# Causal attention: scores and maxima from float32r parts in two 64-row tiles of the array

## The chip, the cores and the metric

The program runs on one core of a Trainium2 chip. The metric is the device time of one execution in microseconds, here the median of three runs. The granted TensorE clock is given as a share of 2.4 GHz: 1.00 is 2.4 GHz and 0.50 is 1.2 GHz.

## What is computed

A stack of four stages over 1024 rows of 512 numbers: a mixture-of-experts layer, a causal attention layer, the same mixture-of-experts layer again, and two further layers. The change touches only the causal attention, whose core is

```python
q = _rope(q, cos, sin)
k = _rope(k, cos, sin)
k = jnp.repeat(k, Q_PER_KV, axis=2)          # 8 key heads serve 32 query heads
scores = jnp.einsum('bqhd,bkhd->bhqk', q, k) * SM_SCALE
scores = jnp.where(mask[None, None], scores, jnp.finfo(scores.dtype).min)
probs = jax.nn.softmax(scores, axis=-1)
ctx = jnp.einsum('bhqk,bkhd->bqhd', probs, v).reshape(B, S, HIDDEN)
```

with 1024 positions, a head width of 16, 8 groups of 4 query heads that share one key and one value head, and a mask that is plain causality at this length. All is float32.

## The kernel before

The causal layer has three blocks, each with one hand-written instruction stream for each engine and semaphores between them. The line numbers are those of the profile.

**The projection** (L1475 to L1676). TensorE makes the queries, keys and values, 128 features by 512 positions in a unit. Of 12 units, 10 hold queries or keys. Each is turned by its position (ScalarE, VectorE, `rotate` on TensorE, GpSimd's sum at L1505) and then split into three bfloat16 parts whose sum is the float32 value: ScalarE casts the first (L1596), GpSimd subtracts it (L1512), ScalarE casts the second (L1600), VectorE subtracts the third (`third`, L1642). SyncE writes the three parts to DRAM (`causal_parts`, L1486). After the seventh write it loads the first group's keys (L1492). The block ends for every engine when SyncE has seen all ten writes land (L1494).

**The core** (L1742 to L2035), a loop over the 8 groups. Scores are taken with six stacked products of parts: `Q_PART` and `K_PART` name the pairs, each of 16 rows, so a product contracts 96 rows. It needs the row maximum before the exponential, and takes every product twice:
- `maximum` (L1864), with the queries as weights: 128 queries by up to 512 keys into one of three banks `mx`; VectorE adds the causal mask and takes the maximum (L2016), or the plain maximum for keys that lie wholly before (L2011). 48 of these make a group.
- `split_maxima` (L1774 to L1788, GpSimd) negates the maxima and splits them into three bfloat16 parts; `turn_maxima` (L1872) transposes them; ScalarE copies them out (L1962); GpSimd's own queue puts them as rows 96 to 98 under the queries (L1794). The keys have ones there.
- `scores` (L1882), with the keys as weights: 128 keys by up to 512 queries, 99 rows, into one of three banks `sc`. ScalarE takes the exponential (L1977) into `prob`; where the block lies on the diagonal GpSimd sets the rest to zero (L1808).
- `values` (L1899): `prob` times the value head, float32, four heads side by side in four 32-column tiles of the array.

A group has 12 steps of four scores. The scores of group g and the maxima of group g + 1 stand in turn, and the values of the step before stand between the third and the fourth score:

```python
for h in range(QPK):
    scores(g, u, h)
    if more:
        maximum(g + 1, UPS * u + h)
    if h == 2 and u >= 1:
        values(g, u - 1)
```

The last group has no maxima to take (`more` is False). The maxima of group 0 stand alone ahead of the loop. TensorE and SyncE run the middle six groups in a hardware loop (`Fori`). SyncE loads a group's keys and queries into place in `ks` and `qs`, which hold all eight groups; the first group's queries are loaded by SyncE and ScalarE at the start of this block (`first_queries`, L1738), and the others follow one after the other as fast as they land (L1748, L1750).

**The output** product and residual follow in the third block.

Of the kernel before, what the change touches and what calls it, by code (L numbers as in the profile page):

```python
# [14 lines left out]
P = 128  # L15
# [1389 lines left out]
def causal_attention_layer(m, name, split):  # L1405
# [8 lines left out]
    Q_PART = (0, 0, 1, 0, 1, 2)  # L1414
    K_PART = (0, 1, 0, 2, 1, 0)
    STACK = len(Q_PART) * HD
    MROWS = 3
    with ExitStack() as outer:
# [3 lines left out]
        parts_dram = nc.dram_tensor(f"{name}_parts", [3, QK_ROWS, S], BF16, kind="Internal").ap()  # L1422
        v_all, ks, ident = m.v_all, m.ks, m.ident_half
        consts, stack_in, ones_done = sem("consts"), sem("stack_in"), sem("ones_done")
# [3 lines left out]
        with ExitStack() as ctx:  # L1428
# [3 lines left out]
            def pb(what, shape, dt=F32):  # L1432
# [13 lines left out]
            rest = [sb(f"rest{s}", [P, CH]) for s in range(2)]  # L1446
            NPB = 4
            part = [sb(f"part{s}", [P, 3, CH], BF16) for s in range(NPB)]
# [10 lines left out]
            turned_done, p1_done, rest_done, p2_done, p3_done = (  # L1459
                sem("turned_done"), sem("p1_done"), sem("rest_done"), sem("p2_done"), sem("p3_done"))  # L1460
# [7 lines left out]
            KEYS = [r for r, n in enumerate(TURN) if n % FEATS == 0]  # L1468
            HALF_T = T // NCH
# [5 lines left out]
            with nc.Block() as block:  # L1475
                @block.sync
                def _(sp):
                    sp.dma_start(b_qkv[:, :], m.dram["b_qkv"]).then_inc(c_in, 16)
                    sp.dma_start(cos[:, :], m.dram["cos"]).then_inc(c_in, 16)
                    sp.dma_start(sin[:, :], m.dram["sin"]).then_inc(c_in, 16)  # L1480
                    m.clear_stale(sp)
                    for r, n in enumerate(TURN):
                        c, j = divmod(n, FEATS)
                        row = j * P
                        sp.wait_ge(p3_done, r + 1)
                        sp.dma_start(parts_dram[:, row:row + P, c * CH:(c + 1) * CH].rearrange("a p s -> p a s"),  # L1486
                                     part[r % NPB][:, :, :]).then_inc(part_out[r % NPB], 16)
# [9 lines left out]
                def _(pool):  # L1497
                    rstd_gpsimd(m, pool, nm)
                    for n in range(UNITS + 3):
                        if n - 1 in number:  # L1500
                            r = number[n - 1]
                            pool.wait_ge(sin_done, r + 1)
                            if r >= 2:
                                pool.wait_ge(rest_done, r - 1)
                            nc.gpsimd.tensor_tensor(turned[r % 2][:, :], with_cos[r % 2][:, :], with_sin[r % 2][:, :],  # L1505
                                                    ALU.add).then_inc(turned_done, 1)
                        if n - 2 in number:
                            r = number[n - 2]
                            pool.wait_ge(p1_done, r + 1)
                            if r >= 2:  # L1510
                                pool.wait_ge(p3_done, r - 1)
                            nc.gpsimd.tensor_tensor(rest[r % 2][:, :], turned[r % 2][:, :], part[r % NPB][:, 0, :],  # L1512
                                                    ALU.subtract).then_inc(rest_done, 1)
# [48 lines left out]
                def _(act):  # L1562
# [16 lines left out]
                    nc.scalar.copy(ident[:, :], m.ident[:, :]).then_inc(consts, 1)  # L1579
# [3 lines left out]
                    for n in range(UNITS + 4):  # L1583
# [7 lines left out]
                        if n - 2 in number:  # L1591
# [4 lines left out]
                            nc.scalar.copy(part[r % NPB][:, 0, :], turned[r % 2][:, :]).then_inc(p1_done, 1)  # L1596
                        if n - 3 in number:
                            r = number[n - 3]
                            act.wait_ge(rest_done, r + 1)
# [680 lines left out]
```

## Time and profile before

| | us |
|---|---|
| median of three runs | 1276.73 (1274.5 to 1277.15) |
| the profiled execution | 1276.3 |
| its span, first to last instruction | 1274.5 |
| mean granted TensorE clock | 0.924 |

The profile is of one execution. Its page gives each engine's busy time, the span in 40 slices and the costliest groups of instructions; its trace can be asked for a stretch (busy time of each engine, granted clock, share of the 16 DMA engines), for the instructions in order of time, and for who waited for whom. Matmuls are pipelined, so one lasts longer in the records than it holds the engine: what it holds is read from the distance between starts.

### The profile page before, as it was taken

The numbers are of one execution on the slowest core, as the hardware profiler recorded it, in microseconds if no ns is written. First come the engines' busy times: TensorE is split into PE (matmuls) and PEld (weight loads), VectorE is DVE, ScalarE is ACT, GpSimd is POOL, SyncE is SP. The second block draws the span as 40 slices with busy tenths as digits, with TensorE's granted clock in tenths as the row PEclk, the third lists the DMA queues.
The fourth block names the chain that finished last, engine by engine and source line by source line (L and its number), as shares of the span: only waits on it lengthen the run. The fifth ranks groups of instructions, "written<-read, shape, count | busy, mean of one in ns | idle before, by whom it ended". The sixth has DMA issues, their size and how long they took to land. (4 is left out here: it accounts for less than half of the span.)

```text
span 1274.5 us, 21579 instructions
## 1 busy us (share of the span) xinstructions
PE 1097.4 (86%) x5654; PEld 717.9 (56%) x5655; DVE 905.9 (71%) x1775; ACT 704.8 (55%) x1218; POOL 566.7 (44%) x582
## 2 busy tenths in 40 slices
PE   4969999999194899999997787999999947878597
PEld 3847777777182233333333675677777735467454
DVE  5869888887575888888860666888888847444632
ACT  3238787887143177777775131787888824424142
POOL 4335666664556244443331225566666545140200
PEclk9979999999596599999998888999999977989889
DMA  9367899764615550000000183789995561000001
GB/s 351 114 220 185 218 243 286 174 114 60 192 50 155 104 99 19 1 1 1 1 1 1 63 309 111 236 196 258 275 222 103 83 156 67 1 1 1 0 1 66
DMA packets 62798, 151.01 MB, mean 118 GB/s; under 512 B 12224, under 2 KB 17024, under 8 KB 58240
## 3 DMA queue, kind: packets, MB, share of 16 engines
q1 hardware_dynamic: 37440, 95.17, 22.3%
q0 software_dynamic: 22592, 50.27, 20.3%
q10 hardware_dynamic: 2688, 4.65, 1.1%
q8 instruction: 34, 0.56, 0.2%
q14 instruction: 44, 0.36, 0.1%
HBM read 104.89 MB, written 44.97 MB: 118 GB/s over the span
## 5 line engine op out<-in xcount | busy, mean ns | idle before, releaser
L811 POOL DMA_INDIRECT moe_acc_rows<-xn,moe_token_of x94 | 208.0, 2213 | 146.3 <-ACT xn L886 131.1
L923 DVE TENSOR_TENSOR moe_w_lo<-moe_raw,moe_w_hi 128x1536 fp32r<-128x1536 f32 x94 | 165.4, 1759 | 62.9 <-ACT moe_w_hi L874 62.7
L1977 ACT ACTIVATE causal_prob<-causal_sc 128x512 f32<-128x512 f32 (+3 forms) x384 | 166.8, 492 | 70.3 <-PE causal_sc L1882 69.7
L874 ACT CAST moe_w_hi<-moe_raw 128x1536 fp32r x94 | 138.7, 1475 | 78.0 <-issue 76.4
L1864 PE MATMUL causal_mx<-ks,causal_qs 96*128 (+4 forms) x384 | 131.4, 353 | 23.0 <-DMA causal_qs<-causal_parts 16.5
L831 PE MATMUL moe_gu<-moe_w_hi,xt_hi 128*128 128x512 f32 x282 | 148.4, 526 | 0.6 <-DVE moe_w_lo L923 0.6
L1882 PE MATMUL causal_sc<-causal_qs,ks 99*128 (+3 forms) x384 | 120.2, 333 | 1.9 <-ACT causal_prob L1977 1.7
L831 PE MATMUL moe_gu<-moe_w_hi,xt_lo 128*128 128x512 f32 x282 | 111.8, 396 | 0.0
L831 PE MATMUL moe_gu<-moe_w_lo,xt_hi 128*128 128x512 f32 x282 | 110.9, 393 | 0.0
L826 PE MATMUL moe_gu<-moe_raw,xn 128*128 x188 | 98.0, 603 | 5.0 <-ACT moe_w_hi L874 5.0
L1808 POOL TENSOR_SCALAR_AFFINE_SELECT causal_prob<-causal_prob 128x512 f32<-128x512 f32 x64 | 40.9, 639 | 115.9 <-ACT causal_prob L1977 115.5
L1899 PE MATMUL causal_po<-causal_prob,causal_v_now 128*32 128x512 f32 (+3 forms) x768 | 81.8, 498 | 9.9 <-POOL causal_prob L1808 9.4
L1882 PEld LDWEIGHTS causal_sc<-causal_qs,ks 99*128 (+1 forms) x384 | 36.4, 97 | 88.9 <-ACT causal_prob L1977 36.7
L2011 DVE TENSOR_REDUCE causal_top_low<-causal_mx 128x1 f32<-128x512 f32 x128 | 80.7, 682 | 7.1 <-PE causal_mx L1864 6.7
L2016 DVE CUSTOM_DVE_ANT_0 causal_mx<-causal_mx,causal_no_later 128x512 f32<-128x512 f32 (+3 forms) x128 | 59.6, 519 | 28.1 <-PE causal_mx L1864 26.7
L1864 PEld LDWEIGHTS causal_mx<-ks,causal_qs 96*128 (+1 forms) x384 | 37.8, 99 | 71.0 <-issue 27.7
L831 PEld LDWEIGHTS moe_gu<-moe_w_hi,xt_hi 128*128 128x128 f32 x282 | 53.6, 190 | 34.1 <-issue 21.6
L105 POOL TENSOR_SCALAR var_eps<-mean_var 128x1 f32<-128x1 f32 x24 | 9.3, 387 | 140.5 <-DVE mean_var L91 140.5
L2016 DVE CUSTOM_DVE_ANT_0 causal_mx<-causal_mx,causal_no_later,causal_top_low 128x512 f32<-128x512 f32 (+3 forms) x128 | 65.3, 553 | 8.9 <-PE causal_mx L1864 8.9
L831 PEld LDWEIGHTS moe_gu<-moe_w_lo,xt_hi 128*128 128x128 f32 x282 | 53.8, 191 | 29.9 <-issue 21.6
L897 ACT CAST xt_hi<-moe_tx 128x384 fp32r<-128x384 f32 x94 | 45.2, 480 | 29.6 <-PE moe_tx L840 25.7
L831 PEld LDWEIGHTS moe_gu<-moe_w_hi,xt_lo 128*128 128x128 f32 x282 | 53.4, 189 | 12.3
(317 smaller groups left out, 2724.5 us busy)
## 6 DMA issues: line engine op xcount, KB each, us to landing
moe_raw<-in_w_gu SPq DMA_DIRECT2D x34, 1024.0 KB, 6.1
moe_raw<-in_w_down SPq DMA_DIRECT2D x34, 512.0 KB, 8.2
causal_qs<-causal_parts SPq DMA_DIRECT2D x45, 128.0 KB, 3.6
moe_acc_rows<-moe_zeros SPq DMA_DIRECT2D x2, 2304.0 KB, 14.7
moe_acc_rows<-x SPq DMA_DIRECT2D x18, 256.0 KB, 2.0
moe_xn_rows<-xn SPq DMA_DIRECT2D x2, 2048.0 KB, 10.7
x<-moe_acc_rows SPq DMA_DIRECT2D x16, 256.0 KB, 6.8
xn<-moe_acc_rows ACTq DMA_DIRECT2D x16, 256.0 KB, 7.2
```

The source lines that it names most:

```text
L811: pool.indirect_dma_start(acc_rows[a], bass.IndirectOffsetOnAxis(ap=token_of[:, b - 3:b - 2].bitcast(U32), axis=0), out_rows[(b - 3) % OUT ...
L826: nc.tensor.matmul(gu[s][:, :], xt_plain[s][:, k, :], raw[:, bass.ds(at + k * 2 * FI, 2 * FI)], start=(k == 0), stop=False)
L831: last = nc.tensor.matmul(gu[s][:, :], xt(half, s, k), part[s][:, k - PLAIN, :], start=False, stop=(k == KT - 1 and half is m.xt_lo))
L874: nc.scalar.copy(w_hi[1 - s][:, :, :], raw[:, bass.ds(at + SPLIT_AT, GU_COLS - SPLIT_AT)].rearrange("p (k n) -> p k n", k=SPLIT)).then_inc ...
L897: nc.scalar.copy(m.xt_hi[:, ks, tokens], tx[s][:, PLAIN * P:KT * P].rearrange("p (k c) -> p k c", k=SPLIT)).then_inc(tx_hi, 1)
L923: nc.vector.tensor_tensor(w_lo[1 - s][:, :, :], raw[:, bass.ds(at + SPLIT_AT, GU_COLS - SPLIT_AT)].rearrange("p (k n) -> p k n", k=SPLIT), ...
L1864: nc.tensor.matmul(mx[i % BANKS][:, 0:w], qs[0:STACK, bass.ds(at, P)], ks[0:STACK, bass.ds(gn * S + kc * CH, w)], start=True, stop=True).t ...
L1882: nc.tensor.matmul(sc[b][:, o:CH], ks[0:STACK + MROWS, bass.ds(g * S + kb * P, P)], qs[0:STACK + MROWS, bass.ds(g * QG + (h * S + c * CH + ...
L1899: last = nc.tensor.matmul(po[2 * HD * h:2 * HD * (h + 1), o:CH], v_now[:, kb, :], prob[u % 2][:, h, o:CH], start=(kb == 0), stop=(kb == (c ...
L1977: nc.scalar.activation(prob[u % 2][:, h, o:CH], sc[(u * QPK + h) % BANKS][:, o:CH], ACT.Exp, scale=SCALE).then_inc(exp_done, 1)
L2011: nc.vector.tensor_reduce(top_low[:, t - TC, h:h + 1], found, AX.X, ALU.max).then_inc(mx_read, 1)
L2016: nc.vector.tensor_tensor_reduce(found, found, no_later[:, CH - w:CH], 1.0, least, ALU.add, ALU.max, top[:, t, h:h + 1]).then_inc(mx_read, 1)
```

## The change

Queries and keys are now split into two parts instead of three. The parts are float32r (a float32 that TensorE takes in a reduced precision), and three products of parts are stacked instead of six, so the contraction is 48 rows (50 with the two rows of maxima). The stacks lie twice in the memory: rows 0 to 49 serve the scores, rows 64 to 111 the maxima, so the two kinds of product use the two halves of the array. Both `keys` and `qs` hold two groups instead of eight (`g % 2`). SyncE loads each stack for itself: the scores' stack of group g + 1 when group g - 1 has made its scores, the maxima's stack of group g + 2 when group g's maxima are made. All stacks of group 0, and the maxima's stack of group 1, are now loaded in the projection block. The loops over groups on TensorE and SyncE are written out; ScalarE keeps its loop. The maxima are split into two parts; they are turned as float32.

```diff
-    Q_PART = (0, 0, 1, 0, 1, 2)
-    K_PART = (0, 1, 0, 2, 1, 0)
-    STACK = len(Q_PART) * HD
-    MROWS = 3
+    Q_PART = (0, 0, 1)
+    K_PART = (0, 1, 0)
+    MROWS = 2
+    MAX_AT = 2 * HD
+    SCORE_ROWS = slice(0, 3 * HD + MROWS)
+    MAXIMA_ROWS = slice(64, 64 + 3 * HD)
+    IN_SCORES = (0, HD, 2 * HD + MROWS)
+    IN_MAXIMA = (64, 64 + HD, 64 + 2 * HD)
...
-        parts_dram = nc.dram_tensor(f"{name}_parts", [3, QK_ROWS, S], BF16, kind="Internal").ap()
+        parts_dram = nc.dram_tensor(f"{name}_parts", [2, QK_ROWS, S], F32, kind="Internal").ap()
...
+        def load_keys(eng, rows, g, done):
+            at = g % 2 * S
+            for a, row in enumerate(rows):
+                eng.dma_start(ks.bitcast(F32)[row:row + HD, at:at + S],
+                              parts_dram[K_PART[a], g * HD:(g + 1) * HD, :]).then_inc(done, 16)
...
-            part = [sb(f"part{s}", [P, 3, CH], BF16) for s in range(NPB)]
+            part = [sb(f"part{s}", [P, 2, CH], F32R) for s in range(NPB)]
...
-                            for a in range(len(Q_PART)):
-                                sp.dma_start(ks[a * HD:(a + 1) * HD, 0:S], parts_dram[K_PART[a], 0:HD, :]).then_inc(stack_in, 16)
+                            load_keys(sp, IN_MAXIMA, 0, for_maxima_in)
+                            load_keys(sp, IN_SCORES, 0, for_scores_in)
+                        if r == QUERIES[-1] + 1:
+                            for k in QUERIES:
+                                sp.wait_ge(part_out[k % NPB], 16 * (k // NPB + 1))
+                            load_queries(sp, IN_MAXIMA, 0, for_maxima_in)
+                        if r == len(TURN) - 1:
+                            load_queries(sp, IN_SCORES, 0, for_scores_in)
+                            sp.wait_ge(for_maxima_in, 16 * LOADS)
+                            load_keys(sp, IN_MAXIMA, 1, for_maxima_in)
+                            load_queries(sp, IN_MAXIMA, 1, for_maxima_in)
...
-                            nc.gpsimd.tensor_tensor(rest[r % 2][:, :], turned[r % 2][:, :], part[r % NPB][:, 0, :],
-                                                    ALU.subtract).then_inc(rest_done, 1)
+                            nc.gpsimd.tensor_tensor(part[r % NPB][:, 1, :], turned[r % 2][:, :], part[r % NPB][:, 0, :].bitcast(F32),
+                                                    ALU.subtract).then_inc(part_lo_done, 1)
...
-                            nc.scalar.copy(part[r % NPB][:, 1, :], rest[r % 2][:, :]).then_inc(p2_done, 1)
...
-                    def third(n):
-                        r = number[n]
-                        dve.wait_ge(p2_done, r + 1)
-                        nc.vector.tensor_tensor(part[r % NPB][:, 2, :], rest[r % 2][:, :], part[r % NPB][:, 1, :],
-                                                ALU.subtract).then_inc(p3_done, 1)
...
-            NEG_OPS = (4, 4)
+            NEG_OPS = (2, 2)
...
-                    for a in range(0, len(Q_PART), 2):
-                        first_queries(sp, a)
...
-                    with sp.Fori(1, KV) as g:
-                        sp.wait_ge(stack_in, g * (16 * LOADS) - 16 * LOADS // 2)
-                        load(g)
...
+                    for g in range(KV - 1):
+                        if g:
+                            sp.wait_ge(sc_done, g * NS * QPK)
+                        load(IN_SCORES, g + 1, for_scores_in)
...
+                        if g + 2 < KV:
+                            sp.wait_ge(mx_done, (g + 1) * NMU)
+                            load(IN_MAXIMA, g + 2, for_maxima_in)
...
-                        nc.tensor.matmul(mx[i % BANKS][:, 0:w], qs[0:STACK, bass.ds(at, P)],
-                                         ks[0:STACK, bass.ds(gn * S + kc * CH, w)], start=True, stop=True).then_inc(mx_done, 1)
+                        at = gn % 2 * QG + h * S + t * P
+                        key = gn % 2 * S + kc * CH
+                        nc.tensor.matmul(mx[i % BANKS][:, 0:w], q_r[MAXIMA_ROWS, at:at + P], k_r[MAXIMA_ROWS, key:key + w],
+                                         start=True, stop=True).then_inc(mx_done, 1)
...
-                        nc.tensor.matmul(sc[b][:, o:CH], ks[0:STACK + MROWS, bass.ds(g * S + kb * P, P)],
-                                         qs[0:STACK + MROWS, bass.ds(g * QG + (h * S + c * CH + o), CH - o)],
+                        nc.tensor.matmul(sc[b][:, o:CH], k_r[SCORE_ROWS, key:key + P], q_r[SCORE_ROWS, at + o:at + CH],
                                          start=True, stop=True).then_inc(sc_done, 1)
...
-                    with pe.Fori(1, KV - 1) as g:
-                        group(g, False, True)
-                    group(KV - 1, False, False)
+                    for g in range(KV):
+                        group(g, g == 0, g < KV - 1)
```

`load` in the new core block waits for the same stack's load before it, then calls `load_keys` and `load_queries` (three DMAs each). `load_queries` moves 64 rows of 4 KB for each of the three parts. `Q_PART` has three entries, so `LOADS` is 6.

The change moves DMA issues on SyncE. At the seam of projection and core, SyncE's order was (`causal_parts` is the DRAM copy of the parts; a row that ends in x3 is three issues):

```order
L1486 DMA causal_parts<-causal_part 128x3x512 x7
L1492 DMA ks<-causal_parts 16x1024 x6
L1486 DMA causal_parts<-causal_part 128x3x512 x3
L1475 UNCONDITIONAL_BRANCH
L1743 UNCONDITIONAL_BRANCH
L1738 DMA causal_qs<-causal_parts 16x4x1024 x3
L1757 DMA causal_no_later<-in_later 128x512
L1758 DMA causal_wd_raw<-in_w_dense 128x1024
```

and is now, where the second branch row again ends the projection block:

```order
L1511 DMA causal_parts<-causal_part 128x2x512 x7
L1440 DMA causal_keys<-causal_parts 16x1024 x6
L1511 DMA causal_parts<-causal_part 128x2x512
L1446 DMA causal_qs<-causal_parts 16x4x1024 x3
L1511 DMA causal_parts<-causal_part 128x2x512 x2
L1446 DMA causal_qs<-causal_parts 16x4x1024 x3
L1440 DMA causal_keys<-causal_parts 16x1024 x3
L1446 DMA causal_qs<-causal_parts 16x4x1024 x3
L1499 UNCONDITIONAL_BRANCH
L1749 UNCONDITIONAL_BRANCH
L1756 DMA causal_wd_raw<-in_w_dense 128x1024
```

The three queries' loads of the maxima moved from behind the block's end to behind the eighth write, and nine more issues stand between the last write and the block's end.

On GpSimd, at the head of the core block, the split of the maxima was

```order
L1774 TENSOR_SCALAR causal_neg<-causal_top 128x16
L1779 CAST causal_neg_parts<-causal_neg 128x4x4
L1782 TENSOR_TENSOR causal_left<-causal_neg,causal_neg_parts 128x16
L1785 CAST causal_neg_parts<-causal_left 128x4x4
L1788 TENSOR_TENSOR causal_neg_parts<-causal_left,causal_neg_parts 128x4x4
L1794 DMA causal_qs<-causal_neg_turned 1x4x512 x3
```

and is now

```order
L1777 TENSOR_SCALAR causal_neg<-causal_top 128x16
L1782 CAST causal_neg_parts<-causal_neg 128x4x4
L1785 TENSOR_TENSOR causal_neg_parts<-causal_neg,causal_neg_parts 128x4x4
L1791 DMA causal_qs<-causal_neg_turned 1x4x512 x2
```

two operations and one DMA shorter, twice in each group. TensorE's order of scores, maxima and values inside a group is the same as before.

## Rows read from the trace of the kernel before

**Rows 1.** The page: busy us (share of the span) xinstructions, by engine.
```profile
PE 1097.4 (86%) x5654; PEld 717.9 (56%) x5655; DVE 905.9 (71%) x1775; ACT 704.8 (55%) x1218; POOL 566.7 (44%) x582
```
**Rows 2.** Stretches: length, PE, PEld, DVE, ACT, POOL busy, clock, DMA share, GB/s.
```profile
409.92:438.93 29.01, 23.25 (x56) 5.55 (x57) 24.66 (x80) 0.57 (x1) 4.30 (x14) 0.50 0.62 123
...
627.32:658.73 31.41, 30.09 (x210) 11.34 (x209) 27.04 (x84) 22.32 (x52) 12.07 (x26) 1.00 0.01 1
658.73:686.60 27.87, 22.36 (x158) 6.63 (x156) 1.78 (x6) 21.59 (x51) 9.34 (x18) 1.00 0.00 1
```
**Rows 3.** In order of time, a step of group 7: start, length, engine.
```profile
676.63 1.07 PE L1899 MATMUL causal_po<-causal_prob,causal_v_now 128*32 128x512 f32 x8
677.63 0.77 PE L1882 MATMUL causal_sc<-causal_qs,ks 99*128 99x384 bf16 x3
678.00 1.96 ACT L1977 ACTIVATE causal_prob<-causal_sc 128x384 f32<-128x384 f32 x4 [0.55 <-PE causal_sc L1882]
678.56 0.64 POOL L1808 TENSOR_SCALAR_AFFINE_SELECT causal_prob<-causal_prob 128x512 f32<-128x512 f32 x1 [4.33 <-ACT causal_prob L1977]
```
**Rows 4.** Who waited for whom in group 6: us, times, longest.
```profile
PEld causal_mx L1864 <- DVE causal_top_low L2011: 1.5, 5, 0.4
```
**Rows 5.** TensorE in order of time, bfloat16 scores and maxima; the last row follows values.
```profile
512.22 0.38 PE L1882 MATMUL causal_sc<-causal_qs,ks 99*128 x1
512.44 0.38 PE L1864 MATMUL causal_mx<-ks,causal_qs 96*128 x1
...
645.62 0.39 PE L1882 MATMUL causal_sc<-causal_qs,ks 99*128 x1
```
**Rows 6.** SyncE, GpSimd, VectorE in order of time, end of the projection.
```profile
393.35 1.15 POOL L1512 TENSOR_TENSOR causal_rest<-causal_turned,causal_part 128x512 f32<-128x512 f32 x1
395.86 2.71 POOL L1512 TENSOR_TENSOR causal_rest<-causal_turned,causal_part 128x512 f32<-128x512 f32 x2
396.48 3.87 SPq L1486 DMA_DIRECT2D causal_parts<-causal_part  x3
398.15 1.80 DVE L1642 TENSOR_TENSOR causal_part<-causal_rest,causal_part 128x512 bf16<-128x512 f32 x2 [1.69 <-ACT causal_part L1600]
403.36 1.30 SPq L1738 DMA_DIRECT2D causal_qs<-causal_parts  x3
409.92 8.63 PE L1864 MATMUL causal_mx<-ks,causal_qs 96*128 96x512 bf16 x18 [16.49 <-DMA causal_qs<-causal_parts]
```
**Rows 7.** Stretches again: all DMA engines busy; later groups loading.
```profile
404.00:410.00 6.00, 0.08 (x1) 0.12 (x2) 0.00 (x0) 1.49 (x2) 6.00 (x1) 0.50 1.00 212
420.00:470.00 50.00, 45.08 (x226) 14.19 (x224) 42.42 (x126) 22.55 (x51) 15.05 (x30) 0.77 0.52 101
```
**Rows 8.** In order of time, from the last maximum of group 0 to the scores.
```profile
437.85 0.20 POOL L1785 CAST causal_neg_parts<-causal_left 128x16 bf16<-128x16 f32 x1
438.13 0.22 POOL L1788 TENSOR_TENSOR causal_neg_parts<-causal_left,causal_neg_parts 128x16 bf16<-128x16 f32 x1
438.41 0.59 PE L1872 MATMUL causal_small<-ident_half,causal_neg_parts 128*12 128x128 bf16 x4 [2.02 <-POOL causal_neg_parts L1788]
```
**Rows 9.** TensorE, a later layer: 32-row tiles, then column tiles, then float32r.
```profile
1074.14 1.14 PE L1078 MATMUL butter_ups<-butter_t_in,up 32*128 32x512 f32 x8
...
1098.78 1.07 PE L1088 MATMUL butter_dn<-butter_hid,down 128*32 128x512 f32 x8
1099.78 0.50 PE L1055 MATMUL butter_io<-gather_spread,butter_d_hi 128*128 128x512 f32 x1
1100.12 0.40 PE L1055 MATMUL butter_io<-gather_spread,butter_d_lo 128*128 128x512 f32 x1
1100.35 0.40 PE L1055 MATMUL butter_io<-gather_spread,butter_d_hi 128*128 128x512 f32 x1
```
**Rows 10.** Weight loads by line: busy us, mean ns.
```profile
L1882 PEld LDWEIGHTS causal_sc<-causal_qs,ks 99*128 x288 | 27.6, 97 | 62.8 <-issue 32.4 <-ACT causal_prob L1977 16.3
L831 PEld LDWEIGHTS moe_gu<-moe_w_hi,xt_hi 128*128 128x128 f32 x282 | 53.6, 190 | 34.1 <-issue 21.6 <-DVE moe_w_lo L923 4.7
```

More of the change, by code:

```diff
@@ L1402, in _, with causal_attention_layer @@
             next_normal(m, dve, T - 1)
-def causal_attention_layer(m, name, split):
+def causal_attention_layer(m, name):
     nc = m.nc
@@ L1420, in sem, with load_queries @@
             return m.semaphore(f"{name}_{what}")
-        parts_dram = nc.dram_tensor(f"{name}_parts", [3, QK_ROWS, S], BF16, kind="Internal").ap()
-        v_all, ks, ident = m.v_all, m.ks, m.ident_half
-        consts, stack_in, ones_done = sem("consts"), sem("stack_in"), sem("ones_done")
+        parts_dram = nc.dram_tensor(f"{name}_parts", [2, QK_ROWS, S], F32, kind="Internal").ap()
+        v_all = m.v_all
+        ks = outer.enter_context(nc.sbuf_tensor(f"{name}_keys", [P, 2 * 2 * S], BF16))[:, :]
+        QG = QPK * S
+        LOADS = 2 * len(Q_PART)
+        qs = outer.enter_context(nc.sbuf_tensor(f"{name}_qs", [P, 2 * 2 * QG], BF16))
+        no_later = outer.enter_context(nc.sbuf_tensor(f"{name}_no_later", [P, CH], F32))
+        no_later_in = sem("no_later_in")
+        q_f, q_r, k_r = qs[:, :].bitcast(F32), qs[:, :].bitcast(F32R), ks.bitcast(F32R)
+        for_scores_in, for_maxima_in, ones_done = sem("for_scores_in"), sem("for_maxima_in"), sem("ones_done")
+        def load_keys(eng, rows, g, done):
[3 more added lines that the diff above has]
+                              parts_dram[K_PART[a], g * HD:(g + 1) * HD, :]).then_inc(done, 16)
+        def load_queries(eng, rows, g, done):
+            at = g % 2 * QG
+            for a, row in enumerate(rows):
+                eng.dma_start(q_f[row:row + HD, at:at + QG].rearrange("d (h s) -> d h s", h=QPK),
+                              parts_dram[Q_PART[a], KV * HD + g * QPK * HD:KV * HD + (g + 1) * QPK * HD, :].rearrange(
+                                  "(h d) s -> d h s", h=QPK)).then_inc(done, 16)
         dense_in, wd_half, wd_ready, x_biased = sem("dense_in"), sem("wd_half"), sem("wd_ready"), sem("x_biased")
@@ L1582, in _ @@
                     act.wait_ge(c_in, 48)
-                    for n in range(UNITS + 4):
+                    for n in range(UNITS + 2):
                         if n < UNITS:
@@ L1664, in _ @@
                     lo(T - 1)
-                    for n in range(2, UNITS + 4):
+                    for n in range(2, UNITS + 1):
                         if n in number:
@@ L1698, in causal_attention_layer @@
             top_low = sb("top_low", [P, TC, QPK])
-            no_later = sb("no_later", [P, CH])
             neg = sb("neg", [P, TC, QPK])
-            left = sb("left", [P, TC, QPK])
-            neg_parts = [sb(f"neg_parts{h}", [P, TC, MROWS, QPK], BF16) for h in range(NCH)]
-            neg_turned = [sb(f"neg_turned{h}", [MROWS * QPK, CH], BF16) for h in range(NCH)]
+            neg_parts = [sb(f"neg_parts{h}", [P, TC, MROWS, QPK], F32R) for h in range(NCH)]
+            neg_turned = [sb(f"neg_turned{h}", [MROWS * QPK, CH]) for h in range(NCH)]
             prob = [sb(f"prob{s}", [P, QPK, CH]) for s in range(2)]
@@ L1940, in _ @@
                     pe.sem_inc(out_turn, 1)
-                    pe.wait_ge(consts, 1)
                     for i in range(NMU):
@@ L1986, in group @@
                                 read_maxima(g + 1, 0)
-                    for a in range(1, len(Q_PART), 2):
-                        first_queries(act, a)
                     nc.scalar.activation(warm[:, :], m.ident[0:1, 0:1], ACT.Exp).then_inc(exp_done, BANKS)
@@ L2181, in program @@
             else:
-                layers[stage](m, f"{stage}{n}", *([split] if stage == "causal" else []))
+                layers[stage](m, f"{stage}{n}")
             if stage == "causal":
+                split.close()
                 early.close()
```

82 lines of the change are left out of this document (27 added, 55 removed).

## The prediction

> **What bounds the kernel now.** I read the page first [rows 1]: TensorE is busy 86% of the span, but that is an average over layers, and the change touches only 366 to 687 us. So I cut this stretch where its parts begin [rows 2]. The prologue, in which group 0's maxima stand alone, lasts 29.0 us; a middle group 31.4 us; group 7, which takes no maxima, 27.9 us.
>
> Those last two rows are the experiment that the kernel makes by itself. Group 6 differs from group 7 by the 48 maxima on TensorE, their 25 us on VectorE (27.04 against 1.78 busy) and one more turning of maxima. All that costs only 31.41 - 27.87 = **3.5 us**. TensorE's busy share falls from 96% to 80% and the group is hardly shorter, so the engine is not what mostly bounds it.
>
> What does is a ring, seen in a step of group 7 [rows 3]: the values of the step before (1.07 us in the records, 1.00 to the next start) hold TensorE, the step's fourth score follows at 677.63, its exponential starts at 678.00 after ScalarE has been idle for 0.55 us, and after a diagonal block GpSimd's mask (0.64 us) stands before the next values. The maxima lengthen this ring where TensorE's stream is full: starts are 0.22 us apart [rows 5], so a pair of score and maximum takes 0.44. VectorE is second: 27.0 of 31.4 us, and 1.5 us of weight loads wait for it [rows 4].
>
> In front of the core there is an idle stretch [rows 6]: the block ends near 403.3, the first queries are loaded then, and the first maximum starts at 409.92, after TensorE has been idle for 16.5 us.
>
> **The change, part by part.** The sum is against the profiled execution, 1276.3 us (0.4 under the median of 1276.7).
>
> *Earlier first maximum.* The queries' loads move into the projection. What is left is the end of that block. What ends last there is the chain of splits behind the products, and in it GpSimd. Its last subtraction ends at 398.57, VectorE's last third part at 399.95, the last write is issued by 400.35 [rows 6]. Now GpSimd's result is the last part, so the write is issued about 1.4 us earlier, near 398.9. But SyncE then issues nine more loads ahead of the block's end, at 0.43 us each (three take 1.30 [rows 6]): 3.9 us, to 402.8, and in their midst it waits for the maxima's queries. These are 768 KB, issued near 395, when GpSimd's eighth subtraction (393.35 plus 1.15 [rows 6]) has been written, behind that write of 512 KB; at 212 GB/s, the rate with all DMA engines busy [rows 7], both take 6 us, so they land near 401 and SyncE is done near 403.5. The block thus ends where it did, 403.4 to 404.0, and the first maximum starts then: 409.9 - 403.5 = **6.4 us less**. Bounds: 7.5 if nothing of SyncE's shows, 3 if the loads take twice as long.
>
> *Shorter split.* Two of five GpSimd operations go, 0.28 us from start to start [rows 8], and TensorE waits for the last at both halves in the prologue: 1.1 us less. Against that eight transposes become float32 at half clock (four take 0.59 us there now [rows 8]), and the maxima are float32r; with VectorE busy 24.7 of 29.0 us [rows 2], little of it shows. **0.3 less**, bounds 1.1 less and 1.5 more. In the later groups the split has slack: nothing there.
>
> *Groups 0 to 6, the overlap.* A score sits in rows 0 to 49 and a maximum in rows 64 to 111, so the two may run together. The trace has row tiles in another layer: eight records, which are four float32 products of 512 columns in four 32-row tiles, take 1.14 us together [rows 9], where a column-tiled set of four takes 1.07. So tiles in different rows do overlap. The ceiling is what the maxima cost in all, 3.5 us. Not won are the turning (0.59 us at half clock [rows 8], so some 0.4 here) and what VectorE holds back; of the 1.5 us of waits for it I take 0.9. That leaves 2.2 us a group.
>
> *Groups 0 to 7, the price of float32r.* After a column-tiled product the first float32r product lasts 0.50 us in the records, its followers 0.40 [rows 9]; the first bfloat16 score after values takes as long as the others (0.39 and 0.38 [rows 5]). The weight load is longer by as much, 190 ns against 97 [rows 10]. There are 12 such places in a group, each in the ring: 12 x 0.11 = 1.3 us more. The Trainium skill, page TensorE: Matmul & The Clock Gate, section Weight-path perf modes, states that the fast weight load is not used for float32, and its section on LDWEIGHTS gives columns divided by 1.2 GHz; the trace agrees in direction (97 against 190 ns). By that page two loads of 107 ns make a pair of 128 columns last 0.21 us where products of 0.06 us each do now, an estimate of 0.7 us a group for 8 pairs, and 1272 us in all.
>
> *Narrow float32r products.* No row shows one under 512 columns. At full rate they cost nothing more. At float32's rate (four times the columns' time, as the 1.07 us for 512 [rows 9] shows) a 128-column score would last 0.16 us longer, and in the two steps of 128 columns it stands in the ring about three times: 0.5. I take 0.2, nearer to the float32r rows than to float32's.
>
> So a group of 0 to 6 changes by -2.2 + 1.3 + 0.2 = **-0.7 us** (bounds -2.2 and +3), seven by -4.9. Group 7 only pays: **+1.5**.
>
> *What costs nothing.* The parts lose a cast on ScalarE and `third` on VectorE in each of 10 units; TensorE covers them in the projection. The memset of ones shrinks to a quarter of its columns, and nobody waits for it. Written-out loops: no gap stands between groups 6 and 7 or inside the loop. Loads: a group's stacks are now 1.92 MB instead of 0.98, each with most of a group (31 us) to land; at 101 GB/s [rows 7] that is 19 us. Bound if that cover fails: 0 to 4 us in all.
>
> Sum: -6.4 - 0.3 - 4.9 + 1.5 = -10.1, so 1276.3 - 10.1 = **1266 us**.
>
> **The rivals.**
> 1. *The overlap and the longer loads cancel.* For it: the ring, not TensorE's throughput, sets most of the group, and the float32r load is in the ring at every step. Against: 3.5 us are there to be had. Then -6.4 - 0.3 + 1.5 gives 1271.
> 2. *The load is hidden.* If the weights of the next tile load while the other tile works, the 1.3 us vanish and groups 0 to 6 win 2.2 us each: -6.7 - 15.4 gives 1254. The Trainium skill, same page, section Packing small matmuls, has this rule: a weight load overlaps running matmuls only when its row group differs. Against it here: after the values, which use all rows, the other tile does not help, and the ring's load stands just there.
> 3. *Slower: no overlap of the two halves.* If scores and maxima still run one after the other, each group pays 1.3 for the first loads, 0.015 us for each of 72 products' worth of 512 columns (float32r starts are 0.23 apart [rows 9], bfloat16 0.22 [rows 5]) = 1.1, and the longer loads before its 16 products of 128 columns, 16 x 0.09 = 1.4; of 3.8 some 3 show. 7 x 3 + 1.5 - 6.7 = +16 gives 1292. It decides from +0.75 us a group on, where it eats the 5.2 that the rest gives. For it: no row shows float32r in row tiles. Against: rows 9.
> 4. *Loads late.* Twice the bytes, and SyncE waits for scores and maxima in one queue. If a group waits 1.5 us for its stack, seven groups eat the gain: 1276. For it: DMA is at 0.52 share with half the bytes. Against: in groups 2 to 7 the engines are idle (0.01 [rows 2]).
>
> **How the numbers follow.** The forecast has 0.45, rival 1 0.23, rival 2 0.12, rival 3 0.13, rival 4 0.07. A measurement of this kernel can tell 0.2% (2.6 us) from no change. Faster: 0.45 + 0.23 + 0.12 = 0.80, less 0.01 for edges; same: rival 4's middle, 0.06; slower: 0.15. The range leaves out most of rival 3 and half of rival 2: 1256 to 1280.
>
> **What would show it.** The first maximum at 403 to 404 us; groups 0 to 6 at 30.7 us, group 7 at 29.4; starts of a score and its maximum some ns apart; the first score after values at 0.50 us; no wait of TensorE for stacks. I am wrong if pairs start 0.23 us apart (rival 3), if group 7 stays at 27.9 (rival 2), or if TensorE's waits name the loads (rival 4).

## The result and the profile after

The changed kernel takes **1349.6 us** (median of 4 runs, 1342.9 to 1351.3) against 1276.6 for the kernel before on the same chip: a ratio of 1.0565, 95% interval 1.0527 to 1.0603. That is 73 us slower, where 10 us faster was forecast and 1280 was the upper end. All of it lies in the core. The profiled execution's span is 1346.9 us.

The page's slices of the whole span show where. A slice is 33.7 us; TensorE's busy share is the first row, its granted clock the second, and the core is slices 13 to 23.

```profile
PE   5969999994768987898799878799999984978697
PEclk9989999997785766887695589799999995989989
```

Before, the clock was 1.00 without a break from 442.8 us, 3.9 us into group 0, to the end of group 7 (1.00 in both groups of [rows 2]). Now it is between 0.5 and 0.9 there, though the engine is about as busy. The stretches of [rows 2] again, by the same columns: the prologue, a group in the middle (group 3), group 6 and group 7.

```profile
405.52:435.14 29.62, 27.33 (x56) 14.20 (x57) 25.13 (x80) 1.72 (x3) 4.06 (x9) 0.50 0.68 111
555.31:596.49 41.18, 32.91 (x212) 14.88 (x212) 27.49 (x84) 22.21 (x52) 12.04 (x22) 0.78 0.38 50
681.97:715.29 33.32, 31.30 (x211) 13.52 (x211) 27.07 (x84) 22.11 (x52) 10.16 (x20) 0.92 0.19 32
715.29:757.75 42.46, 41.97 (x158) 16.57 (x158) 1.78 (x6) 22.07 (x51) 8.45 (x15) 0.50 0.00 1
```

Two things are to be seen. Group 7 takes no maxima, waits for no DMA (share 0.00), and lasts 42.46 us instead of 27.87: its clock is 0.50 and TensorE is busy all the time. Group 3 has, beside a clock of 0.78, 8.3 us in which TensorE is idle (32.91 of 41.18). What it waits for stands in the page's costliest groups of instructions (busy, mean ns | idle before, releaser):

```profile
L1880 PE MATMUL causal_sc<-causal_qs,causal_keys 50*128 50x512 f32 (+3 forms) x384 | 151.3, 488 | 32.6 <-DMA causal_qs<-causal_neg_turned 30.2
```

30.2 us of idle time end with `causal_neg_turned`, the two rows of maxima that GpSimd's queue puts under the queries: not with the stacks. In group 2 these two transfers of 8 KB were issued at 520.5 and 521.1, and the first score of step 4 starts at 530.94. The trace's answer for that line in group 2, and the score in order of time:

```profile
DMA to landing us min/median/max: 9.8/9.9/10.0
...
530.95 0.79 PE L1880 MATMUL causal_sc<-causal_qs,causal_keys 50*128 50x512 f32 x1 [7.70 <-DMA causal_qs<-causal_neg_turned]
```

SyncE had issued 12 loads of stacks and one of weights from 511.6 to 517.5, 2.4 MB, just ahead of them. None of GpSimd's 64 packets starts before 528.4: from 520.6 to 528.4 the DMA engines move 427 packets of SyncE's queue and none of GpSimd's.

The change does do what it says. At the start of group 6, in order of time on TensorE:

```profile
682.25 0.39 PE L1880 MATMUL causal_sc<-causal_qs,causal_keys 50*128 50x512 f32 x1
682.26 0.39 PE L1860 MATMUL causal_mx<-causal_keys,causal_qs 48*128 48x512 f32 x1
682.50 0.50 PE L1880 MATMUL causal_sc<-causal_qs,causal_keys 50*128 50x512 f32 x1
...
683.56 0.50 PE L1880 MATMUL causal_sc<-causal_qs,causal_keys 50*128 50x512 f32 x1
683.56 0.50 PE L1860 MATMUL causal_mx<-causal_keys,causal_qs 48*128 48x512 f32 x1
```

In these rows a score and its maximum start 0.01 us apart or less and the next score follows 0.25 us later; before, each of the two took 0.22 [rows 5]. Of the 336 scores of groups 0 to 6, 267 have a maximum that starts within 0.02 us; the others start further apart. The first score after the values lasts 0.50, as forecast.

### The profile page after: what moved, and what is told of

It is laid out like the page before. It is cut to its first block and busy times, and to the rows that moved or that the text cites. A ratio compares the mean times of both kernels' runs of the same rounds, so it can differ in the third digit from the quotient of the medians.

```text
span 1346.9 us, 20270 instructions
## 1 busy us (share of the span) xinstructions
PE 1150.2 (85%) x5654; PEld 761.7 (57%) x5655; DVE 898.7 (67%) x1765; ACT 697.7 (52%) x1207; POOL 544.5 (40%) x534
## 5 line engine op out<-in xcount | busy, mean ns | idle before, releaser
L1880 PE MATMUL causal_sc<-causal_qs,causal_keys 50*128 50x512 f32 (+3 forms) x384 | 151.3, 488 | 32.6 <-DMA causal_qs<-causal_neg_turned 30.2
L1860 PE MATMUL causal_mx<-causal_keys,causal_qs 48*128 48x512 f32 (+3 forms) x384 | 161.2, 503 | 20.2 <-PEq L1499 14.4
L1880 PEld LDWEIGHTS causal_sc<-causal_qs,causal_keys 50*128 50x128 f32 x384 | 78.8, 237 | 147.4 <-ACT causal_prob L1973 78.2
L1896 PE MATMUL causal_po<-causal_prob,causal_v_now 128*32 128x512 f32 (+3 forms) x768 | 109.4, 652 | 4.0 <-POOL causal_prob L1805 3.7
L1860 PEld LDWEIGHTS causal_mx<-causal_keys,causal_qs 48*128 48x128 f32 x384 | 80.8, 233 | 40.8 <-DVE causal_top_low L2005 15.0
L831 PEld LDWEIGHTS moe_gu<-moe_w_lo,xt_hi 128*128 128x128 f32 x282 | 53.6, 190 | 29.8 <-issue 21.6
```

Of the source, the lines that this page charges most:

```text
L831: last = nc.tensor.matmul(gu[s][:, :], xt(half, s, k), part[s][:, k - PLAIN, :], start=False, stop=(k == KT - 1 and half is m.xt_lo))
L1860: nc.tensor.matmul(mx[i % BANKS][:, 0:w], q_r[MAXIMA_ROWS, at:at + P], k_r[MAXIMA_ROWS, key:key + w], start=True, stop=True).then_inc(mx_d ...
L1880: nc.tensor.matmul(sc[b][:, o:CH], k_r[SCORE_ROWS, key:key + P], q_r[SCORE_ROWS, at + o:at + CH], start=True, stop=True).then_inc(sc_done, 1)
L1896: last = nc.tensor.matmul(po[2 * HD * h:2 * HD * (h + 1), o:CH], v_now[:, kb, :], prob[u % 2][:, h, o:CH], start=(kb == 0), stop=(kb == (c ...
```

## The experiments

Two losses were to be told apart, and each had a rival. **The late rows**: small transfers of maxima wait behind bulk loads issued just ahead of them. **The clock**: it is granted less because the products use few rows of the array, or because they are float32r, or because the stalls bring it down. Steps below are counted from 0; step 4 is the first of the second half. Each ratio is to the kernel before.

### 1. Later loads

```diff
                         if g:
-                            sp.wait_ge(sc_done, g * NS * QPK)
+                            sp.wait_ge(sc_done, g * NS * QPK + C0 * QPK + 1)
                         load(IN_SCORES, g + 1, for_scores_in)
```

> Of the changed kernel: the next group's stacks of the scores are asked for only when the first score of step 4 has run, so 1.1 MB of loads no longer stand ahead of the small transfers of the maxima's rows. Theory A (two separate losses: these rows come late, and TensorE's clock is granted less in the core whatever the transfers do): the step before the second half starts falls from 6.5 to 9.7 us to about 3.5 in groups 1 to 5, 5 x 5.5 = some 27 us in all, so about 1322 us, and group 7 stays at 42 us with a granted clock of 0.5. Theory B (the stalls are what makes the clock fall): with the stalls gone the clock stays at 1.00 from 440 to 690 us, groups last 31 and group 7 29 us, so about 1266 to 1276. Theory C (the rows were late for another reason, such as the split or the turning at half clock): the step stays above 6 us and the time within 10 us of 1349.

Measured: **1313.2 us**, ratio 1.0296 (1.0261 to 1.0331), 36.3 below the changed kernel. The stall is gone: step 3 of groups 1 to 5 lasts 1.6 to 2.1 us instead of 6.5 to 9.7, which is 32 of the 36 us, and the two rows that step 4 of group 2 waits for land in 1.7 us. The two rows of the next pair are now the ones behind the loads, and take up to 9.7 us; nobody waits for them. But the clock still falls: its mean in groups 1 to 6 is 0.83 instead of 0.77. The landing of those two rows, then group 2 and group 7:

```profile
DMA to landing us min/median/max: 1.7/1.7/1.8
...
508.31:539.22 30.91, 29.01 (x210) 13.06 (x212) 27.07 (x84) 22.16 (x52) 12.01 (x22) 1.00 0.54 83
680.10:721.78 41.68, 40.61 (x158) 15.76 (x158) 1.78 (x6) 22.09 (x51) 8.43 (x15) 0.54 0.00 1
```

Theory A holds, with 36 us where 27 were expected. Group 2 happened to have the full clock throughout: it took 30.91 us, half a microsecond less than before.

### 2. Few rows in the old kernel, and its control

```diff
-    Q_PART = (0, 0, 1, 0, 1, 2)
-    K_PART = (0, 1, 0, 2, 1, 0)
+    Q_PART = (0, 0, 1)
+    K_PART = (0, 1, 0)
...
-                    with pe.Fori(1, KV - 1) as g:
+                    for g in range(1, KV - 1):
```

This is the kernel before, all bfloat16, with nothing overlapped. The control has the written-out loop and the moved memset, but all six products.

> Of the kernel before: the stacks hold three of the six products of bfloat16 parts (rows 0 to 47, and three rows of maxima to row 50), so the other three products are left out; TensorE's loops over the groups are written out; the memset of ones stands in the projection. Nothing is float32r in the core and nothing overlaps: a score and a maximum use the same 64 rows of the array. Theory A (few rows of the array at work lower the granted clock): the clock in groups 1 to 7 falls to between 0.5 and 0.8 and group 7 lasts well over 30 us; 1290 to 1340 us in all. Theory B (float32r, the two tiles at once or late transfers lower it): the clock stays at 1.00 as before, groups last 31.4 and group 7 27.9 us, and the time is that of the kernel before, 1276, or up to 5 us less for the shorter loads.

> Of the kernel before: TensorE's loops over the groups are written out and the memset of ones stands in the projection, as in the run with three products of parts, but all six products are kept, so the contractions have 96 and 99 rows again instead of 48 and 51. Theory A (the few rows alone lowered the granted clock there): clock 1.00 from 443 to 688 us, groups of 31.4 us, 1276 us in all, within 3. Theory C (the written-out loops or the memset's place did it): the clock stays at 0.50 and groups last about 53 us, 1438 us in all.

Measured: **1438.6 us** (1.1273, 1.1247 to 1.1298) with three products, **1279.1** (1.0023, 1.0013 to 1.0034) with six. A middle group and group 7 of the run with three, then a middle group of the control:

```profile
597.73:651.02 53.29, 53.05 (x211) 15.42 (x210) 29.59 (x84) 24.43 (x52) 13.89 (x28) 0.50 0.01 1
810.87:849.42 38.55, 37.65 (x157) 8.46 (x156) 1.78 (x6) 21.94 (x51) 9.36 (x18) 0.50 0.00 1
```
```profile
597.91:629.17 31.26, 29.55 (x210) 10.79 (x209) 27.04 (x84) 22.31 (x52) 12.04 (x26) 1.00 0.01 2
```

So few rows alone bring the clock down; neither float32r, nor the two tiles, nor transfers are needed for it: half the rows, hardly any DMA in either stretch (0.01), TensorE busy 53.05 of 53.29 us, and a clock of 0.50 from 401.6 to 862.4 us without a break. That is more than I gave them: 163 us, where 14 to 64 were expected. Whether float32r adds to it this run can't tell; experiment 5 bears on that. The Trainium skill, page TensorE: Matmul & The Clock Gate, section Part 1: The HAM clock gate, describes the clock as going by how busy the engine has lately been. Here it does not follow the busy share of the records: that is 0.99 at the low clock here, and 0.95 at the full clock in the control.

### 3. All 128 rows for the scores

```diff
-    SCORE_ROWS = slice(0, 3 * HD + MROWS)
+    SCORE_ROWS = slice(0, P)
```

with zeros in the unused rows, and the maxima's stack of the next group in the same columns. The sums are then wrong; only the time is of use.

> Of the changed kernel with the later loads: each score contracts all 128 rows, the 50 of its own stack and the rows of the maxima's stack of the next group (with zeros between), so the scores are wrong sums and their exponentials are scaled by a quarter more; a score and a maximum then have no rows apart and cannot overlap. All stays float32r. Theory A (few rows lower the clock): the clock is 1.00 again from 440 to 690 us, group 7 lasts 28 to 30 us, groups 1 to 6 31 to 34, in all 1270 to 1290 us. Theory B (float32r or the traffic lowers it): the clock still alternates, group 7 stays near 42 us, in all 1320 us or more.

Measured: **1614.7 us** (1.266). Neither theory's time. A stretch in the middle (2 us longer than a group, which lasts 79.3), and group 7:

```profile
597.80:679.10 81.30, 81.30 (x219) 32.76 (x211) 30.93 (x84) 25.67 (x53) 12.03 (x22) 0.50 0.21 32
996.14:1025.67 29.53, 26.30 (x156) 11.45 (x156) 1.78 (x6) 21.46 (x50) 8.46 (x15) 0.94 0.01 1
```
```profile
600.53 0.79 PE L1866 MATMUL causal_mx<-causal_keys,causal_qs 48*128 48x512 f32 x1
601.26 0.79 PE L1886 MATMUL causal_sc<-causal_qs,causal_keys 128*128 128x512 f32 x1
```

Group 7, where only scores of 128 rows and values are left, comes to a clock of 0.94 and 29.53 us: float32r by itself does not keep it low. In groups 0 to 6 the maxima of 48 rows still stand between the scores, no longer beside them, and the clock is 0.50. A product of 512 columns then starts every 0.72 us, where the bfloat16 ones of experiment 2 start 0.43 apart at the same clock. The difference, 0.29, is as long as one weight load of float32r (0.285 to 0.287 at this clock): where products of 128 and of 48 rows take turns, it is not hidden. It is not overlapping rows as such that do this: products of 128 rows behind one another, also float32r, start 0.23 apart at the full clock [rows 9], and three such scores in group 7 here take 0.85 us together. What it is about the turns was not tested. The 1614.7 us are thus two costs together, the low clock and the loads.

### 4. Both tiles filled with zeros

```diff
-    SCORE_ROWS = slice(0, 3 * HD + MROWS)
-    MAXIMA_ROWS = slice(64, 64 + 3 * HD)
+    SCORE_ROWS = slice(0, 64)
+    MAXIMA_ROWS = slice(64, P)
```

GpSimd writes the zeros at the start of the projection, which delays the first maximum to 412.6 and 411.5 us, from 406.4 and 405.5. The first version has the later loads of experiment 1; the second keeps the loads where the change puts them.

> Of the changed kernel with the later loads: the two tiles are filled up with rows of zeros, so that scores contract rows 0 to 63 and maxima rows 64 to 127; the result is the same. Theory A1 (it counts how many rows the products name, whatever is in them): 128 rows at once while the two overlap instead of 98, and 64 instead of 50 in group 7; the clock alternates less, the time is 1265 to 1295 us and group 7 below 38 us. Theory A2 (it counts something that zeros do not raise, or only a tile's fixed size): the time stays within 8 us of the 1313 with later loads, and group 7 at 41 to 42 us.

> Of the changed kernel: only the rows of zeros that fill both tiles are added (rows 0 to 63 and 64 to 127), and the loads stay where the change has them, at the start of a group. It completes a square with the changed kernel (1349.6 us), later loads (1313.2) and later loads with full tiles (1292.1, where groups at a clock of 1.00 last 30.9 us). Theory A (two separate losses): the late rows of maxima cost 5 to 6 us at step 3 in groups 1 to 5, some 27 us over the 1292, so 1315 to 1325 us, and the clock is higher than in the changed kernel, though it falls in the stalls, as it did for 6.8 us in group 1 of the run with early queries. Theory D (all comes from the rows, and the late transfers cost little when the clock is up): below 1300 us. Theory E (the stalls alone bring the clock down, full tiles do not help against them): above 1335 us.

Measured: **1292.1 us** (1.0115, 1.0069 to 1.0161) and **1337.6 us** (1.047, 1.0431 to 1.0509). Group 2 and group 7 of the first, group 3 of the second:

```profile
507.24:538.14 30.90, 28.97 (x210) 13.08 (x212) 27.05 (x84) 22.17 (x52) 12.02 (x22) 1.00 0.52 83
662.72:700.32 37.60, 35.76 (x157) 13.80 (x157) 1.78 (x6) 22.06 (x51) 8.43 (x15) 0.65 0.00 1
```
```profile
555.74:596.44 40.70, 30.89 (x211) 13.99 (x212) 27.35 (x84) 22.15 (x52) 11.98 (x22) 0.83 0.36 50
```

Theory A1: rows of zeros count. With 64 and 64 rows at once the clock stays at 1.00 from 459 to 674 us but for 3.4. Group 7 has only 64, and it falls again. The square of the four runs:

| | loads at the group's start | later loads |
|---|---|---|
| 50 and 48 rows | 1349.6 | 1313.2 |
| 64 and 64 rows | 1337.6 | 1292.1 |

The late rows cost 36.3 us in the changed kernel and 45.5 with full tiles. Of the 45.5, 42 stand in step 3 of groups 1 to 5, which lasts 9.7 to 10.2 us each against 1.6. I had expected 5 to 6 us a group of it, and that is why the second run lies 13 us above theory A's range. The clock also falls to 0.50 for 10 to 14 us behind each stall, where without the stalls it falls only once, for 3.4; so stalls bring it down too, but that adds only the 3 to 4 us that are left. The full tiles gain 21 us with later loads and 12 without, both net of the 6 us by which the core starts later.

### 5. bfloat16 in the two tiles

```diff
-            part = [sb(f"part{s}", [P, 2, CH], F32R) for s in range(NPB)]
+            part = [sb(f"part{s}", [P, 2, CH], BF16) for s in range(NPB)]
```

and likewise for the stacks and the maxima's rows.

> Of the changed kernel with the later loads: the parts, the stacks and the maxima's rows are bfloat16 instead of float32r, in the same rows of the same two tiles, so the result is coarser (the low parts are cut to bfloat16 and the third is left out) and each load has half the bytes. Theory A (the rows decide, not the type): the clock still alternates between 0.5 and 1.0 in groups 0 to 6 and is 0.5 in group 7, which lasts 36 to 42 us; 1290 to 1315 us in all. Theory B (float32r lowers the clock when it is spread over two tiles): the clock stays at 1.00 and the time is 1255 to 1270 us.

Measured: **1274.1 us** (0.9984, 0.9971 to 0.9997), between the ranges of the two theories. The clock does fall in bfloat16 too, but little in groups 1 to 6, which last 29.8 to 31.2 us. Group 2 and group 7:

```profile
493.85:523.67 29.82, 26.52 (x210) 8.57 (x212) 26.91 (x84) 22.21 (x52) 12.08 (x22) 0.96 0.25 53
647.34:686.24 38.90, 38.00 (x158) 8.49 (x158) 1.78 (x6) 21.94 (x51) 8.49 (x15) 0.50 0.00 1
```

Group 7 is theory A's case: a clock of 0.50 with bfloat16 and 50 rows. In groups 1 to 6 the type matters as well, against theory A: the mean clock is 0.95 here and 0.83 with float32r in the same rows (experiment 1). The two runs differ by 39 us, and at the full clock float32r costs only some 12 of them (1.5 a group, experiment 7). So few rows cost much more in float32r than in bfloat16 here. Whether that comes from the type, from the bytes of its loads or from how the products then follow each other stays open.

### 6. Only the first queries loaded early

The kernel before, with the first group's queries loaded behind the queries' last write; the second version also loads the table of later keys in the projection and asks for groups 4 to 7 one at a time.

```diff
+                        if r == QUERIES[-1] + 1:
+                            for k in QUERIES:
+                                sp.wait_ge(part_out[k % NPB], 16 * (k // NPB + 1))
+                            for a in range(len(Q_PART)):
+                                first_queries(sp, a)
...
-                    for a in range(0, len(Q_PART), 2):
-                        first_queries(sp, a)
```

> Of the kernel before: only the first group's queries (six loads of 128 KB in bfloat16) are loaded during the projection, into columns of the keys that groups 4 to 7 use later; those groups' loads wait until group 0 is through. Both theories on the seam: if SyncE's queue and the landing decide, the first maximum starts near 405 us instead of 409.9, as in the changed kernel (405.5), and the time is 4 to 5 us less, 1272; if the gain is taken back by the loads of later groups or by the memset's place, within 1 us of 1276.

> Of the kernel before, as in the run with only the first queries loaded early (1281.9 us, where VectorE's first maximum waited from 407 to 409 us for the table that covers later keys, and step 4 of group 1 lasted 5.1 instead of 2.15 us behind the burst of four groups' loads): the table is now loaded at the start of the projection, and the stacks of groups 4 to 7 are asked for one group at a time, after step 4. Theory A (small transfers of the maxima's rows wait behind bulk loads that are issued just ahead of them): group 1 lasts 31.5 us instead of 37.4, the first maximum's reading follows at once, and the time is 1272 to 1274 us, 2 to 4 below the kernel before. Theory C (something else held group 1 up): group 1 stays above 35 us and the time above 1278.

Measured: **1281.9 us** (1.0053, 1.0033 to 1.0073), which neither theory gave, and **1277.4 us** (1.0009, 0.9998 to 1.0019). The first maximum comes at 406.80 and 407.36 instead of 409.92. In the first version VectorE waits for the table of later keys until 409.06, and group 1 stalls behind the burst of four groups' loads. Its group 1; then group 0 and group 1 of the second:

```profile
468.78:506.14 37.36, 33.30 (x210) 11.78 (x209) 27.85 (x84) 22.66 (x52) 13.86 (x28) 0.91 0.44 90
```
```profile
436.38:469.55 33.17, 32.16 (x193) 11.41 (x193) 26.54 (x80) 22.49 (x50) 12.23 (x22) 0.86 0.02 3
469.55:500.96 31.41, 30.12 (x211) 11.25 (x209) 27.04 (x84) 22.39 (x52) 13.90 (x28) 1.00 0.17 34
```

Pacing the loads mends group 1: theory A for the transfers, in a kernel with none of the change's tiles. But the expected 2 to 4 us do not come. Group 0 now lasts 33.17 us instead of 31.28: the clock rises at 445.5, before at 442.8, so this earlier start of the core is spent at the low clock. In the first version the clock rises at 441.5, group 0 lasts 31.47 us, and most of its 1.6 us of earlier start is kept until group 1 stalls. So an earlier start is not always lost. What sets the moment of the rise I did not test.

### 7. The change at its best

Later loads, full tiles, the zeros written in ten pieces between GpSimd's operations, and in group 7:

```diff
+                        rows = slice(0, P) if g == KV - 1 and u >= 3 else SCORE_ROWS
...
-                        nc.tensor.matmul(sc[b][:, o:CH], k_r[SCORE_ROWS, key:key + P], q_r[SCORE_ROWS, at + o:at + CH],
+                        nc.tensor.matmul(sc[b][:, o:CH], k_r[rows, key:key + P], q_r[rows, at + o:at + CH],
```

> Of the changed kernel with later loads and full tiles: the zeros are written in ten pieces between GpSimd's operations of the projection instead of at its start (which had put the first maximum at 412.6 instead of 405.5 us), and in group 7, when the maxima's keys have been overwritten with zeros, the scores contract all 128 rows from step 3 on; the result is the same. Theory A (rows at work decide): group 7 lasts 30 to 33 us instead of 37.6, the first maximum comes at 405 to 407, and the time is 1276 to 1283 us, so the change at its best is level with the kernel before, since groups of 30.9 against 31.4 us gain only 3 us and group 7 loses 2. Theory C (group 7's clock is low for another reason, such as its idle time): group 7 stays at 37 us and the time above 1283.

> The same for the variant with parts of bfloat16 in the two tiles (1274.0 us, groups of 29.8 us at full clock, group 7 at half clock 38.9), which leaves out the third parts and so computes coarser scores and maxima: tiles filled with zeros, zeros in pieces, 128 rows in group 7 from step 3 on. Theory A: clock 1.00 from about 450 us to the end of group 7, groups 1 to 6 29.8 us, group 7 29 to 31 us, in all 1258 to 1266 us. Theory C: group 7 stays above 37 us, in all 1270 us or more.

Measured: **1278.8 us** (1.0036, 1.001 to 1.0061) in float32r, **1259.7 us** (0.9884, 0.9861 to 0.9908) in bfloat16. A middle group and group 7 of each:

```profile
501.61:532.52 30.91, 29.00 (x211) 13.12 (x212) 27.08 (x84) 22.15 (x52) 11.99 (x22) 1.00 0.55 83
657.06:686.97 29.91, 25.51 (x158) 10.53 (x158) 1.78 (x6) 21.74 (x51) 9.35 (x16) 1.00 0.01 1
```
```profile
519.49:548.88 29.39, 25.91 (x212) 8.48 (x213) 26.90 (x84) 22.10 (x52) 11.98 (x22) 1.00 0.20 35
638.04:666.52 28.48, 22.66 (x158) 6.56 (x158) 1.78 (x6) 21.64 (x51) 9.35 (x16) 1.00 0.00 1
```

Both times lie in theory A's ranges. With 128 rows in use group 7 is at the full clock again, 29.91 us instead of 37.60. The float32r version is the whole change without its two losses, and is still 0.4% slower than the kernel before. The bfloat16 one is 1.2% faster than the kernel before, but it leaves out the third parts, so it is not the same computation.

## Why the prediction was wrong

The 73 us, from the runs: the late rows 36.3 (1349.6 to 1313.2), the few rows of the array 34.4 (1313.2 to 1278.8, by full tiles and 128 rows in group 7), and 2.2 left over. The split depends on the order: with full tiles the late rows cost 45.5. And the 34.4 are what few rows cost in float32r; experiment 5 shows that bfloat16 pays less for them.

**The step that failed** is one that the prediction does not have. It took every duration at the clock of the rows of before, 1.00, and gave the clock neither a term nor a bound. What the runs showed in its place is a clock below 1.00 in every group (0.92 in group 6, 0.78 in group 3, 0.50 in group 7), 42.46 us instead of 27.87 in group 7, and 34.4 us in all. In the trace of before hardly anything that TensorE does has fewer than 96 rows in the array; the 32-row tiles of [rows 9] run four at a time. The change puts a resource to a use that no row shows, and the range should have had that as an unknown.

**Loads at nothing, bounds 0 to 4; rival 4.** This is the second step that failed: the loads' new place cost 36.3 us. The cover was right for the stacks: no wait names them. But what else the loads would stand ahead of was not asked. Before, they were one stream, paced by the landing of each group's and over in group 1 (the last is issued at 475.3); the maxima's rows took 1.7 to 3.9 us to landing beside it in group 0 and 1.6 to 2.0 in group 1. Now up to 2.4 MB are issued at once at the start of a group, and behind them in time come the maxima's rows, 8 KB each on GpSimd's queue: 9.8 to 10.0 us to landing in group 2 against 1.7 free of loads. The Trainium skill, page DMA: Bandwidth & Descriptors, section Queues, rings and completion order, has each DMA engine take its queues in turn, a packet at a time. By that rule GpSimd's packets should have come in among SyncE's once they were issued; in this trace none did from 520.6 to 528.4, while 427 of SyncE's moved. Why they started so late stays open.

**The overlap, -2.2 us a group: right.** Without float32r's price a group takes 29.39 us at the full clock (experiment 7), before 31.42: -2.0. This is of a kernel that also has half the bytes to load, so the overlap was not measured quite alone.

**float32r, +1.3 and +0.2 a group: right in sum.** 30.90 - 29.39 = 1.5 us, all else equal but the bytes of the loads. The two were not told apart, but narrow products are fast: pairs of 128 columns start 0.11 us apart at 606.04 and 606.15 in the changed kernel, and not 0.21, the prediction's estimate for two weight loads one after the other. So a group at the full clock is -0.5 us, forecast -0.7.

**Group 7, +1.5: near at the full clock, wrong in the changed kernel.** There it was +14.6, for the clock. In the best float32r version it is 29.91 - 27.87 = +2.0, of which 1.3 are a wait for GpSimd's zeros that the change does not have; against bfloat16 in the same form (28.48) it is +1.4.

**The earlier first maximum, -6.4: 2.0 us too large, and then mostly lost.** It came at 405.52, 4.4 us earlier: SyncE's last load of queries is issued at 403.91, and the next block's first instructions stand at 405.17. In group 0 the gain is given back, since the clock rises late: 34.20 us even in the best float32r version, against 31.28.

**The shorter split, -0.3:** the prologue is 29.62 us against 29.01, so +0.6. With bfloat16 in the tiles (experiment 5) it is 28.73, so the split gave its 0.3 and float32r's maxima took 0.9.

With these sizes the sum is about 1277, by the best float32r run: 250.5 us for the eight groups against 247.7, and a start 2.4 earlier. That is no gain instead of 10 us, even without the two losses. Rival 3, the one on the slow side (1292), is refuted as a mechanism: a score and its maximum do start together.

## What to carry to other kernels

Before products are packed into row tiles, ask what the clock does with the rows that stay empty: fill both tiles with zeros, and read the granted clock of the stretch, not only the busy share. When bulk loads are moved to a new place, list the small transfers that are issued just behind them, on every queue, and who waits for them. A start gained while the clock is low may be worth nothing: look when the clock rises in the new trace.

## What I had not expected of the hardware

- Half the contraction rows made the same number of products much slower: 1438.6 us against 1279.1, by a clock of 0.50 at a busy share of 0.99.
- Rows of zeros raised the granted clock: 1292.1 us against 1313.2, and group 7 29.9 us against 41.7.
- With few rows in use float32r had a lower clock than bfloat16 in the same rows: 0.83 against 0.95 in groups 1 to 6.
- An 8 KB transfer took 9.8 to 10.0 us behind 2.4 MB on another queue, and 1.7 free of it; none of its packets started in the 7.8 us from its issue to 528.4, while 427 of the other queue moved.
- A weight load of float32r did not show where the other tile worked beside it (pairs 0.25 us apart), and was paid in full where products of 48 and of 128 rows took turns (0.72 instead of 0.43 us at the low clock).
